# Expert layers in tiles of 256 or 128 slots, sorted by group, with a float32 down projection; half of the attention sums on VectorE

## The chip, the cores and the metric

The kernel runs on one core of a Trainium2 chip. The metric is the device time of one execution in microseconds (us); lower is better. Engines are named as in the profile: PE (TensorE), DVE (VectorE), ACT (ScalarE), POOL (GpSimd) and SP (SyncE, which only issues DMAs here).

## The reference

`x` is 32 sequences of 256 tokens of 128 features, 8192 tokens. One block is a half-weighted mixture of experts, then windowed attention, then the same mixture of experts again:

```
x = x + 0.5 * ffn(layernorm(x))
x = x + attn(layernorm(x))
x = x + 0.5 * ffn(layernorm(x))

ffn:   scores = softmax(x @ Wg + bg)              # 8 experts
       the 2 best experts of each token
       h  = gelu(x @ W1[e] + b1[e])               # 128 -> 512, exact gelu
       eo = h @ W2[e] + b2[e]                     # 512 -> 128
       out = sum of the 2 results, each times its probability
attn:  16 heads of 8 features; token s looks at tokens s-8 .. s
       softmax(q . k / 0.56) over these 9, times v, then @ Wo
```

## The kernel before

The 8192 tokens are four **groups** of 2048 (128 partitions x 16 tokens). There are two **passes** over the experts, f = 0 ahead of the attention and f = 1 behind it.

**Expert pass.** Each token of a group is normalised, its gates and its two experts are found (`route`, on PE, DVE and ACT), and two copies of its row are scattered to a DRAM buffer sorted by expert (`scatter_rows`: 32 indirect DMAs of POOL for a group, 128 rows each). Groups are collected in **parts**, `PARTS = ((0, 1), (2, 3))`; a part has its own sorted buffer, `x_sorted0` or `x_sorted1`. When all rows of a part have landed, `plan` has told on DVE which expert and which rows each **tile** of `SLOT_TILE` = 256 slots has. A part of two groups has 39 tiles, 156 in both passes. For each tile, SP issues a transposing load of 256 rows (`load_x`: value load, DMA_TRANSPOSE, then a small load of the rows' ids); four loads may be ahead. PE makes the up projection (`up`: 12 float16 products of 256 columns, three for each quarter of the hidden units, since `x` and `W1` are each a high and a low float16 part). ACT applies gelu into `h_f` in float32 and casts a high part; DVE subtracts it for the low part (`split_h`, two for a tile, L1347). PE makes the down projection (`down`: 24 float16 products of 128 columns, and one for the bias). DVE multiplies by the gate (`take_y`, L1355), and POOL scatters the result to `y_pairs` in token order (`scatter_y`, L572: two indirect DMAs for a tile, 312 in all). A ring of four `y_sb` buffers lies between the last two.

**Behind a part.** `load_y` waits until every result of the part that holds group g is scattered; `combine` adds the two results to `x` in SBUF.

**Attention**, group after group: `prepare` and `make_qkv`, then eight chunks of two tokens per partition. `multiply_keys` (DVE), sums over the features (PE for the first four chunks, DVE for the others), softmax, `prob_value(c)` (DVE, product of 2 x 9 x 128 elements into `prod`, L1176), `add_window(c)` (PE: nine float32 products with the identity, 256 columns each, add the nine positions in PSUM, L856), `take_o(c)` (DVE, divided by the sum), `turn_o`, `project` (PE) and `add_attention(c)` (DVE, L1204).

**Order.** Each engine runs five streams (routing r, rows h or s, experts e or y, attention a, preparation p). Their interleaving is written out by hand in strings, one letter per step (`PE_ORDER` and so on); `take_turns` walks them. An engine executes its instructions in this order, so a wait of one stream holds the others behind it. In the second pass, `scatter_rows` waits after each four DMAs (`BURST`) until they have landed.

## Time and profile before

| | |
|---|---|
| median of 3 runs | 1198.52 us (1195.54 to 1204.46) |
| the profiled execution | 1194.16 us, its span 1192.4 us |
| mean granted PE clock | 0.866 of full speed |
| PE busy | 871.4 us (73% of the span) |
| DVE busy | 766.5 us (64%) |
| ACT busy | 666.7 us (56%) |
| POOL busy | 665.9 us (56%) |
| indirect DMAs of POOL | 256 of rows, 312 of results |

Busy time counts the instructions themselves; the space between two of them is idle time, whether the engine waits for another or for its own sequencer. No engine is busy all along, so the totals alone do not bound the kernel: the stages must be read one by one. The execution's own time stands 1.8 us above its span, and 4.4 us under the median of the runs.

### The profile page before, as it was taken

To read this page: it belongs to the slowest core of one execution; us is meant where nothing else is said; L and a number is where in the kernel's file an instruction comes from. 1 tells how busy PE (TensorE), PEld (TensorE's weight loads), DVE (VectorE), ACT (ScalarE), POOL (GpSimd) and SP (SyncE) were. 2 spreads that over 40 slices of the span, in tenths; PEclk is the share of its full clock that TensorE was granted. 3 is DMA by queue.
4 is the path that set the end of the run, shared out by engine and by line. 5 is a ranking of instruction groups with operands and counts; after the bars stand their busy time and mean duration, and the time that the engine had idled before them with its cause. 6 is when DMAs were issued, how large, how long until landed. Compare 5 with 4: busy or idle time off the path is not lost.

```text
span 1192.4 us, 25209 instructions
## 1 busy us (share of the span) xinstructions
PE 871.4 (73%) x7573; PEld 708.8 (59%) x7573; DVE 766.5 (64%) x1366; ACT 666.7 (56%) x1408; POOL 665.9 (56%) x595
## 2 busy tenths in 40 slices
PE   1633086529898989998877978979998783298991
PEld 1523065318676767877766656657786662187781
DVE  4565344216457789579996898679875472056664
ACT  4533186419779666267714621367628673197890
POOL 2386677777775313206665305636675765676672
PEclk9755599759999999999987978989998887598996
DMA  8421143224457110002142002113214341146656
GB/s 267 127 82 48 52 99 75 74 60 89 111 113 155 56 28 23 10 14 53 29 134 72 16 1 67 33 43 72 58 43 71 74 99 54 47 84 163 147 126 213
DMA packets 168050, 94.86 MB, mean 80 GB/s; under 512 B 138893, under 2 KB 151738, under 8 KB 167156
## 3 DMA queue, kind: packets, MB, share of 16 engines
q1 hardware_dynamic: 149748, 57.54, 20.8%
q0 software_dynamic: 18176, 35.72, 10.3%
q8 instruction: 70, 1.15, 0.4%
q14 instruction: 56, 0.46, 0.1%
HBM read 25.78 MB, written 50.59 MB: 64 GB/s over the span
## 4 chain that ended last, share of the span: by engine, by line
PE 25%; DVE 16%; issue 8%; POOL 8%; DMA 8%; SPq 4%; ACT 3%; POOLq 0%; ACTq 0%; DVEq 0%
POOL x_sorted L555 7%; PE bank L948 6%; PE bank L927 6%; DMA x_sorted<-hl,slots_all 5%; PE bank L856 5%; PE bank L843 4%; DVE prod L1132 3%; DVE h_hl L1347 2%; DVE prod L1143 2%; SPq L440 2%; PE bank L829 2%; DMA y_in<-y_pairs 2%; DVE prod L1176 2%; ACT h_f L738 1%; POOL y_pairs L572 1%
## 5 line engine op out<-in xcount | busy, mean ns | idle before, releaser
L572 POOL DMA_INDIRECT y_pairs<-y_sb,tile_ids x312 | 363.2, 1164 | 281.8 <-issue 242.8
L555 POOL DMA_INDIRECT x_sorted<-hl,slots_all x256 | 294.6, 1151 | 223.1 <-DVE hl L1027 92.4
L738 ACT ACTIVATE h_f<-bank,b_cols 128x256 f32<-128x256 f32 x624 | 261.2, 469 | 142.4 <-PE bank L927 125.9
L927 PE MATMUL bank<-xsT,w_hl 128*128 128x256 f16 x1872 | 250.8, 285 | 83.5 <-DMA xsT<-x_sorted 70.9
L948 PE MATMUL bank<-w_hl,h_hl 128*128 x3744 | 249.4, 224 | 64.2 <-DVE h_hl L1347 64.1
L1347 DVE TENSOR_TENSOR h_hl<-h_f,h_hl 128x512 f16<-128x512 f32 x312 | 212.2, 687 | 110.1 <-ACT h_hl L744 106.8
L948 PEld LDWEIGHTS bank<-w_hl,h_hl 128*128 128x128 f16 x3744 | 218.5, 100 | 88.0 <-issue 70.3
L927 PEld LDWEIGHTS bank<-xsT,w_hl 128*128 x1872 | 182.2, 102 | 117.1 <-issue 90.3
L744 ACT CAST h_hl<-h_f 128x512 f16<-128x512 f32 x312 | 192.9, 618 | 9.9
L856 PE MATMUL bank<-prod,ident 128*128 128x256 f32 x576 | 143.2, 408 | 16.5 <-DVE prod L1176 15.0
L856 PEld LDWEIGHTS bank<-prod,ident 128*128 128x128 f32 x576 | 116.5, 206 | 37.1 <-DVE prod L1176 18.9
L1355 DVE TENSOR_TENSOR y_sb<-bank,tile_ids 128x256 f32<-128x256 f32 x156 | 65.7, 421 | 80.4 <-issue 45.8
L662 ACT COPY qkv<-bank 128x384 f32<-128x384 f32 (+1 forms) x96 | 41.2, 444 | 77.4 <-PE bank L829 37.0
L1132 DVE TENSOR_TENSOR prod<-qkv 128x2304 f32<-128x2304 f32 x32 | 81.5, 2549 | 0.3
L1176 DVE TENSOR_TENSOR prod<-score,qkv 128x2304 f32<-128x2304 f32 x32 | 81.5, 2548 | 0.1
L843 PE MATMUL bank<-prod,ident 128*128 128x288 f32 x256 | 63.9, 407 | 0.4 <-DVE prod L1132 0.4
L938 PE MATMUL bank<-b_hl,ones_b 64*128 x156 | 44.4, 284 | 20.9 <-DVE y_sb L1355 20.7
L843 PEld LDWEIGHTS bank<-prod,ident 128*128 128x128 f32 x256 | 48.2, 190 | 14.7 <-DVE prod L1132 1.0
L647 ACT CAST hl<-xn_r 128x1024 f16<-128x1024 f32 x20 | 20.8, 1039 | 59.9 <-DMA x_sorted<-hl,slots_all 59.9
L1016 DVE TENSOR_TENSOR hl<-xn_r,hl 128x1024 f16<-128x1024 f32 x20 | 24.4, 1222 | 46.1 <-ACT hl L647 46.1
L938 PEld LDWEIGHTS bank<-b_hl,ones_b 64*128 64x128 f16 x156 | 14.5, 93 | 57.7 <-issue 57.1
L829 PE MATMUL bank<-wqkv,xnT_p 128*128 128x384 f32 x128 | 47.0, 492 | 0.0
(151 smaller groups left out, 825.1 us busy)
## 6 DMA issues: line engine op xcount, KB each, us to landing
y_in<-y_pairs SPq DMA_DIRECT2D x24, 512.0 KB, 4.2
y_pairs<-y_sb,tile_ids POOLq DMA_INDIRECT x312
x_sorted<-no_rows SPq DMA_DIRECT2D x32, 144.0 KB
x_sb<-in_L_attn_x SPq DMA_DIRECT2D x4, 1024.0 KB, 6.3
x_sorted<-hl,slots_all POOLq DMA_INDIRECT x256
qkv<-y_pairs SPq DMA_DIRECT2D x8, 512.0 KB, 6.8
xsT<-x_sorted SPq DMA_TRANSPOSE x156
tile_ids<-x_sorted SPq DMA_DIRECT2D x156, 2.0 KB
```

Of the source, the lines that this page charges most:

```text
L555: pool.indirect_dma_start(out=x_sorted[p], out_offset=bass.IndirectOffsetOnAxis(ap=slots_all[:, at:at + 1], axis=0), in_=hl[:, c % 2, i // ...
L572: pool.indirect_dma_start(out=y_pairs, out_offset=bass.IndirectOffsetOnAxis(ap=tile_ids[:, t.n % IDS, i, 0:1].bitcast(U32), axis=0), in_=y ...
L738: ins = act.activation(h_f[:, u % H_RING, c % 2, :], bank[h_banks.uses[u][0]][:, (c % 2) * 256:(c % 2 + 1) * 256], ACT.Gelu, bias=b1_cols[ ...
L744: act.copy(h_hl[:, t.par, 0, 2 * b:2 * b + 2, :], h_f[:, u % H_RING]).then_inc(h_hi, 1)
L829: pe.matmul(prep_bank[k % PREPS][:, 0:3 * D], xnT_p[:, k - RADIUS, 1:1 + P], wqkv[:], start=True, stop=True).then_inc(qkv_done, 1)
L843: ins = pe.matmul(score_bank[c % 2][:, 0:JH * W * HEADS].rearrange("p (n h) -> p n h", h=HEADS), ident[:], products[:, :, d, :], start=(d ...
L856: ins = pe.matmul(score_bank[c % 2][:, 0:JH * D].rearrange("p (j d) -> p j d", d=D), ident[:], prod[:, c % 2, :, w, :], start=(w == 0), st ...
L927: ins = pe.matmul(dst, w_flat[:, bass.ds((e * HC + c) * (2 * P) + ws * P, P)], xsT[:, t.ring, s], start=(n == 0), stop=(n == 2))
L948: ins = pe.matmul(into[:, half, :], h_hl[:, t.par, hs, c, mine], w_flat[:, bass.ds(at + ws * D, D)], start=False, stop=(c == HC - 1 and ws ...
L1132: ins = dve.tensor_tensor(prod[:, prod_of[c]], q_ap.to_broadcast([P, JH, W, D]), windows(lo, D), ALU.mult)
L1176: dve.tensor_tensor(prod[:, c % 2].rearrange("p j w (h d) -> p j w h d", d=DK), score[:, lo:lo + JH].rearrange("p j w (h o) -> p j w h o", ...
L1347: dve.tensor_tensor(h_hl[:, t.par, 1, 2 * b:2 * b + 2, :], h_f[:, u % H_RING], h_hl[:, t.par, 0, 2 * b:2 * b + 2, :], ALU.subtract).then_i ...
```

## The change

- **Parts.** The first pass has one part for each group; the second has (0, 1), (2) and (3). Seven parts, each with its own buffer, its own `plan` and its own eight tails to clear (of 128 rows, where it was 256).
- **Tiles.** An expert's rows are cut into units of 128. Tiles are wide (two units, 256 slots) or half (one unit). A part of one group has 15 wide and 9 half tiles, the part of two groups has 31 and 9: 184 tiles, 121 wide and 63 half, 305 units in all. `plan` has 34 steps for it, where it had 16.
- **Down projection.** `W2` stays in float32, and so does `h_f`, now a ring of six. The cast on ACT and `split_h` on DVE go; `down` has 8 float32 products of 128 columns for a wide tile and 4 for a half one, in place of 24 in float16.
- **Attention.** For the odd chunks (1, 3, 5, 7) of each group the nine positions are added on DVE by halving (4 + 4, 2 + 2, 1 + 1, and the ninth), four instructions of 1024, 512, 256 and 256 elements behind `prob_value(c)`. `add_window` goes for them on PE.
- **Buffers and orders.** The normalised rows of group 3 lie in `xn_r`, not in `y_in`. All five order strings are new.

```diff
-SPARE = 8
-TAIL = SLOT_TILE
+SPARE = 10
+TAIL = P
-PARTS = ((0, 1), (2, 3))
+H_RING = 6
+SPLITS = (((0,), (1,), (2,), (3,)), ((0, 1), (2,), (3,)))
+SUMMED_BY_DVE = (1, 3, 5, 7)
 POOL_ORDER = (
-    "sssssssssyysyyyyyysyysyysssyyyyyyyyyyyyyyyyyyysyyyyyyyyyyyyyyyyyyyyyyyyyyyyyyyyyyyyyyyyyyyyyyssssssssssssssss"
+    "ssssssyyyyyyysyyyyyyyysyyyyyyyysyyyyyyyyyyysyyyyyyyyysysyyyyyyyyyyyyyyyssyyyssyyyyyyyyyyyyyssssyssssyyyyyyyyy"
...
-    HT = [(2 * GROUP * len(gs) - E) // SLOT_TILE + E for gs in PARTS]
+    UNITS = [(2 * GROUP * len(gs) - E) // P + E for gs in PARTS]
+    WIDE = [(n - E) // 2 for n in UNITS]
+    HT = [n - w for n, w in zip(UNITS, WIDE)]
...
 def experts():            # ACT
-                    for b in range(2):
-                        u = 2 * t.n + b
+                    for b in range(t.halves):
+                        u = t.u + b
                         act.wait_ge(h_done, u + 1)
                         if u >= H_RING:
-                            act.wait_ge(h_split, u - (H_RING - 1))
...
+                            act.wait_ge(y_done, tile_of_unit[u - H_RING] + 1)
...
-                        act.copy(h_hl[:, t.par, 0, 2 * b:2 * b + 2, :],
-                                 h_f[:, u % H_RING]).then_inc(h_hi, 1)
...
 def down(t, e):           # PE
                     for c in range(HC):
-                        if c % 2 == 0:
-                            pe.wait_ge(h_split, 2 * t.n + (c // 2 + 1))
-                        at = (e * HC + (c + E * HC)) * (2 * D)
-                        for ws in range(2):
-                            for half in range(2):
-                                mine = slice(half * P, (half + 1) * P)
-                                for hs in range(2 - ws):
-                                    ins = pe.matmul(into[:, half, :], h_hl[:, t.par, hs, c, mine],
-                                                    w_flat[:, bass.ds(at + ws * D, D)], start=False,
-                                                    stop=(c == HC - 1 and ws == half == 1))
+                        if c % t.per == 0:
+                            pe.wait_ge(h_gelu, t.u + (c // t.per + 1))
+                        for half in range(t.halves):
+                            ins = pe.matmul(into[:, half, :], h_part(t, c // t.per)[:, c % t.per, half * P:(half + 1) * P],
+                                            w2_flat[:, bass.ds((e * HC + c) * D, D)], start=False,
+                                            stop=(c == HC - 1 and half == t.halves - 1))
...
 def prob_value(c):        # DVE
+                    if c in SUMMED_BY_DVE:
+                        parts = prod[:, c % 2]
+                        dve.wait_ge(pv_ready, g * CH + (c + 1))
+                        for n in (4, 2):
+                            at.did(dve.tensor_tensor(parts[:, :, 0:n], parts[:, :, 0:n], parts[:, :, n:2 * n], ALU.add))
+                            at.settle()
+                        at.did(dve.tensor_tensor(parts[:, :, 0], parts[:, :, 0], parts[:, :, 1], ALU.add))
+                        at.settle()
+                        at.did(dve.tensor_tensor(parts[:, :, 0], parts[:, :, 0], parts[:, :, W - 1], ALU.add))
+                        yield
...
 def attention(g):         # PE
-                    yield from add_window(c)
-                    yield from add_window(c + 1)
+                    for k in (c, c + 1):
+                        if k not in SUMMED_BY_DVE:
+                            yield from add_window(k)
...
 def experts():            # DVE
-                def split_h(t, b):
-                    u = 2 * t.n + b
-                    dve.wait_ge(h_hi, u + 1)
-                    dve.tensor_tensor(h_hl[:, t.par, 1, 2 * b:2 * b + 2, :], h_f[:, u % H_RING],
-                                      h_hl[:, t.par, 0, 2 * b:2 * b + 2, :], ALU.subtract).then_inc(h_split, 1)
```

**Where the orders differ.** First place: POOL's queue from its first scatter. A row says which DMAs follow one another and how many; `y_pairs` are results, `x_sortedN` the rows of part N. Before:

```order
L555 DMA x_sorted0<-hl,slots_all 36864x144 x64
L555 DMA x_sorted1<-hl,slots_all 36864x144 x8
L572 DMA y_pairs<-y_sb,tile_ids 16384x128 x4
L555 DMA x_sorted1<-hl,slots_all 36864x144 x8
L572 DMA y_pairs<-y_sb,tile_ids 16384x128 x12
```

The same place in the changed kernel:

```order
L579 DMA x_sorted0<-hl,slots_all 18688x144 x32
L579 DMA x_sorted1<-hl,slots_all 18688x144 x16
L596 DMA y_pairs<-y_sb,tile_ids 16384x128 x16
L579 DMA x_sorted1<-hl,slots_all 18688x144 x8
L596 DMA y_pairs<-y_sb,tile_ids 16384x128 x15
L579 DMA x_sorted1<-hl,slots_all 18688x144 x8
L596 DMA y_pairs<-y_sb,tile_ids 16384x128 x8
```

The 39 results of part 0 are now complete with the 103rd DMA; before, part 0 (78 results, of groups 0 and 1) was complete with the 206th.

Second place: the end of POOL's queue, from the last group's rows in the second pass on. Before, then changed:

```order
L555 DMA x_sorted1<-hl,slots_all 36864x144 x4
L572 DMA y_pairs<-y_sb,tile_ids 16384x128 x2
L555 DMA x_sorted1<-hl,slots_all 36864x144 x28
L572 DMA y_pairs<-y_sb,tile_ids 16384x128 x88
```

```order
L579 DMA x_sorted6<-hl,slots_all 18688x144 x8
L596 DMA y_pairs<-y_sb,tile_ids 16384x128 x21
L579 DMA x_sorted6<-hl,slots_all 18688x144 x8
L596 DMA y_pairs<-y_sb,tile_ids 16384x128 x16
L579 DMA x_sorted6<-hl,slots_all 18688x144 x4
L596 DMA y_pairs<-y_sb,tile_ids 16384x128 x17
L579 DMA x_sorted6<-hl,slots_all 18688x144 x12
L596 DMA y_pairs<-y_sb,tile_ids 16384x128 x45
```

The last 32 rows' DMAs now have 54 results among them and 45 behind them, where 2 lay among them and 88 behind them. Ahead of the first of these rows stand 430 DMAs in the changed queue.

Third place: DVE between the chunks of an attention. Before, in group 0:

```order
L1204 TENSOR_TENSOR x_sb<-bank7,x_sb 128x256
L1176 TENSOR_TENSOR prod<-score,qkv 128x2304
L1185 TENSOR_REDUCE ssum<-score 128x128
L1188 RECIPROCAL sinv<-ssum 128x128
L1347 TENSOR_TENSOR h_hl<-h_f,h_hl 128x512
L1355 TENSOR_TENSOR y_sb<-bank3,tile_ids 128x256
L1347 TENSOR_TENSOR h_hl<-h_f,h_hl 128x512 x2
L1195 TENSOR_TENSOR o_sb<-bank6,sinv 128x256
```

and changed:

```order
L1240 TENSOR_TENSOR x_sb<-bank7,x_sb 128x256
L1194 TENSOR_TENSOR prod<-score,qkv 128x2304
L1203 TENSOR_TENSOR prod<-prod 128x2x512
L1203 TENSOR_TENSOR prod<-prod 128x2x256
L1205 TENSOR_TENSOR prod<-prod 128x2x128
L1207 TENSOR_TENSOR prod<-prod 128x2x128
L1213 TENSOR_REDUCE ssum<-score 128x128
L1216 RECIPROCAL sinv<-ssum 128x128
L1396 TENSOR_TENSOR y_sb<-bank3,tile_ids 128x256
L1231 TENSOR_TENSOR o_sb<-bank6,sinv 128x256
```

The three `h_hl` are gone, and four additions stand behind the product. Between the first product with the keys and the last `add_attention`, DVE has 68 `y_sb` (47 wide, 21 half) where it had 38, 16 `hl` where it had 12, 48 BN_STATS where it had 40, 24 additions of results to `x_sb` where it had 16, and two plans where it had one.

## Rows read from the trace of the kernel before

**Rows 1.** The page, busy time and 40 equal slices (tenths of busy time).
```profile
PE 871.4 (73%) x7573; PEld 708.8 (59%) x7573; DVE 766.5 (64%) x1366; ACT 666.7 (56%) x1408; POOL 665.9 (56%) x595
PE   1633086529898989998877978979998783298991
...
POOL 2386677777775313206665305636675765676672
```

**Rows 2.** Busy time by stretch: from:to, length, busy us (instructions) of five engines, clock, DMA.
```profile
160.00:360.00 200.00, 140.39 (x1616) 115.52 (x1615) 87.33 (x154) 129.09 (x270) 154.68 (x144) 0.85 0.40 89
402.00:892.00 490.00, 430.07 (x2837) 343.09 (x2836) 412.25 (x583) 245.08 (x528) 217.13 (x158) 0.94 0.16 43
520.00:600.00 80.00, 70.42 (x675) 58.72 (x673) 75.35 (x107) 56.56 (x114) 41.85 (x30) 0.99 0.16 36
```

**Rows 3.** Timeline of POOL: start us, us, instruction, idle time before it.
```profile
46.81 1.15 POOL L555 DMA_INDIRECT x_sorted<-hl,slots_all  x1 [37.94 <-DVE hl L1027]
...
142.22 0.96 POOL L555 DMA_INDIRECT x_sorted<-hl,slots_all  x1 [0.30 <-issue]
...
199.82 0.95 POOL L555 DMA_INDIRECT x_sorted<-hl,slots_all  x1 [0.30 <-issue]
...
342.12 0.98 POOL L572 DMA_INDIRECT y_pairs<-y_sb,tile_ids  x1 [0.30 <-issue]
...
595.95 2.48 POOL L572 DMA_INDIRECT y_pairs<-y_sb,tile_ids  x1 [1.40 <-issue]
...
974.80 0.96 POOL L555 DMA_INDIRECT x_sorted<-hl,slots_all  x1 [0.30 <-issue]
...
1030.88 0.96 POOL L555 DMA_INDIRECT x_sorted<-hl,slots_all  x1 [0.30 <-issue]
...
1170.50 0.98 POOL L572 DMA_INDIRECT y_pairs<-y_sb,tile_ids  x1 [0.30 <-issue]
```

**Rows 4.** Timeline of DVE.
```profile
352.64 0.69 DVE L1107 TENSOR_TENSOR x_sb<-y_in,x_sb 128x512 f32<-128x512 f32 x1 [0.69 <-DMA y_in<-y_pairs]
...
402.17 2.56 DVE L1132 TENSOR_TENSOR prod<-qkv 128x2304 f32<-128x2304 f32 x1
...
595.03 2.55 DVE L1176 TENSOR_TENSOR prod<-score,qkv 128x2304 f32<-128x2304 f32 x1
...
891.56 0.88 DVE L1204 TENSOR_TENSOR x_sb<-bank,x_sb 128x256 f32<-128x256 f32 x2
```

**Rows 5.** Timeline of SP's queue; these are the moments of issue.
```profile
148.40 1.26 SPq L440 DMA_TRANSPOSE xsT<-x_sorted  x1
...
151.02 1.24 SPq L440 DMA_TRANSPOSE xsT<-x_sorted  x1
...
1033.92 1.23 SPq L440 DMA_TRANSPOSE xsT<-x_sorted  x1
```

**Rows 6.** The chain of waits: start us, us, what.
```profile
1124.10 1.45 PE bank L948 x24
1125.55 1.31 PE bank L927 x12
...
1127.07 1.45 PE bank L948 x24
```

**Rows 7.** Timeline of PE.
```profile
483.72 1.11 PE L873 MATMUL bank<-wo_sb,oT 128*128 128x128 f32 x8
```

**Rows 8.** Groups of instructions: xcount | busy us, mean ns | idle before.
```profile
L948 PE MATMUL bank<-w_hl,h_hl 128*128 x3744 | 249.4, 224 | 64.2 <-DVE h_hl L1347 64.1
L1347 DVE TENSOR_TENSOR h_hl<-h_f,h_hl 128x512 f16<-128x512 f32 x312 | 212.2, 687 | 110.1 <-ACT h_hl L744 106.8
L873 PEld LDWEIGHTS bank<-wo_sb,oT 128*128 128x128 f32 x128 | 18.3, 209 | 2.8 <-ACT oT L674 1.7
L856 PE MATMUL bank<-prod,ident 128*128 128x256 f32 x576 | 143.2, 408 | 16.5 <-DVE prod L1176 15.0
L1016 DVE TENSOR_TENSOR hl<-xn_r,hl 128x1024 f16<-128x1024 f32 x20 | 24.4, 1222 | 46.1 <-ACT hl L647 46.1
```

More of the change, by code:

```diff
@@ L369, in macaron, with sums_before @@
         SCATTERS = J * DMA
+        def sums_before(g, c):
+            return g * (CH - len(SUMMED_BY_DVE)) + sum(k not in SUMMED_BY_DVE for k in range(c))
         def xt(t, n=1):
@@ L714, in routes @@
                     if q == PARTS[0][-1]:
-                        for part in range(2):
-                            round_weights(part)
-                            yield
+                        round_weights()
+                        yield
             def prepares():
@@ new lines, in plan @@
+                did(dve.tensor_tensor(units[:, 0, :], counts[:], units[:, 1, :], ALU.subtract))
+                for k in range(2):
+                    did(dve.tensor_tensor(m.sums[:, k], earlier[0:1, :].rearrange("o (e f) -> o e f", f=E),
+                                          units[:, k, :].rearrange("o (e f) -> o e f", e=1).to_broadcast([1, e1, E]), ALU.mult))
+                did(dve.tensor_reduce(starts[:].rearrange("o k e -> o (k e)"),
+                                      m.sums.rearrange("o k e f -> o (k e) f"), X, ALU.add))
@@ new lines, in plan @@
+                did(dve.tensor_scalar(counts[:, 0:1], starts[:, 0, E:e1], float(2 * WIDE[p]), None, ALU.max))
+                did(dve.tensor_scalar(starts[:, 1, :], starts[:, 1, :], counts[:, 0:1], None, ALU.add))
+                offs = row_off[:, 1:].rearrange("o (k e) -> o k e", k=2)
+                did(dve.memset(row_off[:, 0:1], 0.0))
+                for k in range(2):
+                    did(dve.scalar_tensor_tensor(out=offs[:, k], in0=starts[:, k], scalar=-float(P), in1=start,
+                                                 op0=ALU.mult, op1=ALU.add))
@@ L1294, in plan @@
+                did(dve.tensor_tensor(m.row, m.row, m.row2, ALU.add))
+                did(dve.scalar_tensor_tensor(out=tile_row[:, cols], in0=m.unit, scalar=float(P),
+                                             in1=m.row, op0=ALU.mult, op1=ALU.add))
+                dve.tensor_tensor(tile_expert[:, cols], m.expert, m.expert2, ALU.add).then_inc(plan_ready, 1)
                 yield
```

373 lines of the change are left out of this document (189 added, 184 removed).

## The prediction

> **What bounds the kernel now.** I read the busy shares first [rows 1]: no engine is above 73%, so the whole is not one engine's work but a row of stages, and the slices show them. For the first two slices no experts run. From then to about 360 us POOL's slices read 7 and 6 while PE's fall to 3 in places: POOL is the pace. The stretch from 160 to 360 us gives the price: 144 indirect DMAs in 200 us, 1.39 us each, with 0.30 us between one and the next even when its data are ready [rows 2, 3]. From 402 to 892 us attention runs; there DVE is busy 412 of 490 us (84%) and PE 430 (88%) [rows 2, 4], both in one chain, so neither can be full. The last stage is experts alone: tile after tile, 1.45 us of down products, 1.31 us of up products and 0.21 us of bias, 2.97 us a tile [rows 6].
>
> Three waits join the stages. Attention can't start until part 0 (groups 0 and 1) is complete: POOL's 206th DMA at 342 us, the first result added at 352.6, the first product of attention at 402 [rows 3, 4]. From the last `add_attention` at 892 to the first rows of group 3 it takes 83 us, mostly because the routing steps stand between expert steps; the 32 rows take 56 us, four at a time [rows 3]. And then 39 tiles have to go through before the end: SP's first load of the last part is at 1033.9, 158 us ahead of it [rows 5].
>
> **The change, part by part.**
>
> The start: `plan` now stands ahead of the gates' copy that releases POOL, and has 34 small instructions, so I add 7 us to the first scatter at 46.8 (34 at 0.2 us, an estimate: 256 elements take 0.44, and these have 1 to 216). Part 0 is complete with the 103rd DMA, not the 206th. The 103rd stood at 199.8 in the run before [rows 3]; with 7 us more, 207. From there to the first addition it took 10.5 us (342.1 to 352.6), to the first product another 49.5 [rows 3, 4]; with ACT and PE less full I take 48. Attention starts at 265 us instead of 402. Nothing else in this change is worth as much, 137 us.
>
> Attention itself, on DVE. Its 412 us lose `split_h`: 38 tiles lay in the stretch, two at 0.687 us each, 52 us [rows 8]. They gain the halving: 1024, 512, 256 and 256 elements. A two-input instruction of 1024 elements took 1.22 us [rows 8], of 512 0.69 and of 256 0.44 [rows 4], so 2.8 us a chunk and 45 us for sixteen. 47 wide and 21 half `take_y` at 0.44 and at most that, less the 38 there now, give 10; four more `hl` 5; one more set of statistics 5; eight more additions of results 6; the other plan 7. That makes 412 - 52 + 45 + 33 = 438 us. On PE it loses 16 chunks of nine products, half of 143 us, 72 us [rows 8]. A tile on PE costs 1.31 + 0.95 + 0.21 = 2.5 us when wide and half of it when half: eight float32 products of 128 columns ran in 1.11 us from first start to last end, the last alone being 0.28 of it, so 0.12 us each [rows 7], where 24 in float16 take 1.45. The 30 tiles more cost PE what the cheaper ones save (68 at 2.1 us, 143, against 38 at 3.4, 129), so 430 - 72 + 14 = 372 us. PE stops being a rival to DVE. Its slack and the missing round trip over PE for half of the chunks should cut DVE's idle time of 78 us in this stretch to some 50: the four attentions take 488 us and end at 753. This idle time is the term I know least; at 84% busy as now it would be 521 us, at 95% 461.
>
> POOL beside it. From 265 us, with 145 DMAs done (42 more at 1.39), 285 must go before group 3's last rows, in the new order. At 1.39 us that is 396, and 24 bursts of the second pass wait 2 us each (56 us for 32 rows and two results, 34 at 1.27 being 43), 48: 709 us. But beside attention POOL is slower: between 520 and 600 us 30 DMAs were busy 41.85 us, 1.40, with the 0.30 1.70 us each [rows 2]; one that met a product of 2.55 us on DVE took 2.48 instead of 0.98 [rows 3, 4]. At 1.70 it is 798 us. The halving adds to such instructions, 45 us, the going of `split_h` takes away 52. So POOL comes to that place between 709 and 798, and attention (below) at 793: near a tie, and attention is at the late end, so I let attention decide and keep the other as a rival.
>
> The Trainium skill (SBUF — State Buffer, "Who interferes with whom") says that a DVE instruction with two SBUF inputs contends with GpSimd's reads, and that whichever issues first keeps the other out; this is a rule against the halving. The row of 2.48 us beside the product agrees with it. By the rule the change would be neutral here, as 52 us of such instructions go and 45 come.
>
> The end. From the last `add_attention` to the first rows: 83 us now; in the new order some nine PE steps of experts stand ahead of the routing, and then one or two between its steps, so I take 40 (statistics, 16 normalisations, routing: about 30 us of dependent steps; the bound above is 83). First rows at 793. The 32 rows take 56 us as now; 54 results lie among them at 1.28 us, 69: 918 us. Loads begin 3 us behind (1030.9 to 1033.9) [rows 3, 5]. The last part has 24 tiles, not 39. PE needs 2.5 us for a wide one, POOL 2.6; SP's own queue issued a tile each 2.62 us (148.40 to 151.02) [rows 5] and does so for a half one too, unless the transposing load of 128 rows is issued faster. So 23 x 2.6 = 60 us to the last load, 981; some 6 us for that tile's way over four engines (estimate: 3 to land, and one product stage, gelu, product, gate of under 1 us each). From the last scatter to the end it was 21.9 us [rows 3]; four chunks of two additions at 0.69 go, 5.5 [rows 4], 16.4. Sum 1003.7 us of span, 1005.5 with the 1.8 outside. Against the run of before that is -189: 137 by the earlier start, 2 by attention, 43 by the routing and 76 by the smaller last part, less 69 for the results that now lie among the last rows. I forecast 1005 us; the profiled run lies 4 us under the median, well inside the range.
>
> What costs nothing: ACT loses its casts, and is the bound nowhere (56% busy [rows 1]); if it had been full, they would count. The 56 tails instead of 32, each of half the size, stand in SP's queue ahead of a part's first load, in time that waits for the rows; at the borders in the second pass they may cost up to 10 us each when the rows are already there.
>
> **Rivals.**
> - *Attention runs fuller.* DVE at 95%, the routing in 30 us and 15 us less from first results to first product: 250 + 461 + 30 = 741 us, 52 less, 954 us. For it: PE has slack. Against: 84% is what this chain reached, and POOL must be at its quick end (709).
> - *POOL is the bound beside attention.* `take_y` may not overtake the scatter by more than four tiles, so DVE, which runs attention in the same queue, is held behind POOL. At 1.70 us it comes to group 3's rows at 798, and the 86 DMAs there cost 86 x 1.70 + 16 = 162, not 125: 1005 + 5 + 37 = 1047 us. For it: 285 DMAs at 1.7 fill the time. Against: 1.39 where DVE was not full.
> - *The early start does not come.* SP has the loads of group 0's results behind 30 tile loads, six of them of part 1, whose tails and rows it must wait for. If the queue holds them until 402 us as now, only the end is cheaper: 1194 - 43 - 76 = 1075 us, the results being out of the way by then.
> - *The float32 rule.* Rows show twice the time of float16 for a column: 576 products of 256 columns were busy 143.2 us, 0.25 each [rows 8], 12 in float16 took 1.31, 0.11 each [rows 6]. With four times, a product of 128 columns takes 0.21 us and a wide tile 3.2 on PE: PE is as full as now beside attention (68 tiles at 0.7 more, 420 of 488), DVE back at 84%, +33, and the last part's wide tiles +9: 1047 us. The Trainium skill (FP8 and Floating Point Precision, "TensorE Precision Notes") has it that true float32 takes four passes through the array; the trace has two times, and its measurement decides.
> - *Slower than before.* The down products could fail to hide their weight loads, since here each has new weights: a load of 0.21 and a product of 0.28 in series, 0.49 us [rows 7, 8]. 1220 of them take 598 us against 249 now [rows 8]; PE: 871 - 249 - 72 + 598 = 1148 us, and at 93% busy 1234 us. It passes the time of before from 0.46 us a product. Against it: `project` has new weights for each product too, and ran at 0.12.
>
> **How the numbers follow.** The forecast has 0.50, its own range 970 to 1040 (the attention between 461 and 521 us, the routing 30 to 60). Fuller attention 0.20, POOL 0.15, no early start 0.07, the float32 rule 0.05, slower 0.03. To leave out no more than 2 in 10 the range has to take in 954 and 1047 with their own spread: 935 to 1075. No change within 1%, which is about what a measurement of this kernel can tell, has no case of its own; I give it 0.01, slower 0.03 and faster 0.96.
>
> **What the new profile would show.** The first product of attention near 265 us; the last `add_attention` near 753; DVE in between 88% to 90% busy; POOL without long idle times from 55 to 790 us; down products of a wide tile in 0.95 us; the last part's loads from about 920 us, 2.6 us apart. Wrong would be: attention starting past 300 us, POOL at 1.7 us throughout, DVE waiting on scattered results, or a float32 product dearer than 0.2 us.

## The result, and the profile after

The changed kernel takes 1103.11 us (median of 4 runs, 1100.78 to 1108.01) against 1197.47 us of the kernel before: ratio 0.921, 95% interval 0.917 to 0.926. The forecast was 1005 us with a range of 935 to 1075. The sign was right; the forecast was 98 us too low, and the time lies above the range. The profiled execution has a span of 1102.5 us, 98.8 more than the 1003.7 of the sum. Ratios, here and below, leave out executions that took over 1.5% longer than the fastest of the same kernel, so a few in the table of experiments aren't the quotients of the medians beside them.

The page after, to be read beside [rows 1]: busy time, 40 slices, and then some of its groups.

```profile
PE 878.7 (80%) x6345; PEld 736.0 (67%) x6345; DVE 642.4 (58%) x1305; ACT 498.3 (45%) x1217; POOL 669.1 (61%) x593
PE   1542996899989888987999679689889577992994
...
POOL 3076777667857787466677256367757664574553
...
L963 PE MATMUL bank<-w_sb,h_f 128*128 x2440 | 337.9, 291 | 0.9 <-ACT h_f L758 0.9
...
L871 PE MATMUL bank<-prod,ident 128*128 128x256 f32 x288 | 73.7, 412 | 5.9 <-DVE prod L1194 3.3
```

PE was expected to have less to do than before and has more, 878.7 us for 871.4. The reason stands in the count of L963. The code makes 1220 float32 products there (305 units, four quarters), and the trace has 2440 records. L871 has 288 records for 144 products. So a float32 product is two PE instructions in the trace. The same was to be seen in the kernel before: 576 records at L856 [rows 8] are 32 chunks of nine products, 288.

The chain of waits in the last part, beside [rows 6]: start us, us, what.

```profile
1057.86 0.21 PE bank L957
1058.07 1.98 PE bank L963 x16
1060.05 1.31 PE bank L946 x12
...
1076.50 1.09 PE bank L963 x8
1077.59 0.67 PE bank L946 x12
1078.26 0.16 PE bank L957
```

A wide tile is 1.98 + 1.31 + 0.21 = 3.50 us of PE, dearer than before's 2.97 and not the 2.5 of the forecast. The 16 records of 1.98 us are eight products, 0.25 us each. A half tile is 1.09 + 0.67 + 0.16 = 1.92 us, where the forecast had half of 2.5.

POOL's timeline at the places of [rows 3]: the first row, the 103rd DMA, the first and the last row of the last group, the last result.

```profile
53.86 4.36 POOL L579 DMA_INDIRECT x_sorted<-hl,slots_all  x1 [44.53 <-DVE hl L1043]
...
201.07 0.98 POOL L596 DMA_INDIRECT y_pairs<-y_sb,tile_ids  x1 [0.30 <-issue]
...
862.89 0.97 POOL L579 DMA_INDIRECT x_sorted<-hl,slots_all  x1 [0.30 <-issue]
...
1006.08 0.96 POOL L579 DMA_INDIRECT x_sorted<-hl,slots_all  x1 [0.30 <-issue]
...
1087.75 0.98 POOL L596 DMA_INDIRECT y_pairs<-y_sb,tile_ids  x1 [0.34 <-issue]
```

DVE's timeline, beside [rows 4]: first result added, first product of attention, last `add_attention`.

```profile
212.66 0.69 DVE L1123 TENSOR_TENSOR x_sb<-y_in,x_sb 128x512 f32<-128x512 f32 x1 [0.49 <-DMA y_in<-y_pairs]
...
276.63 2.55 DVE L1148 TENSOR_TENSOR prod<-qkv 128x2304 f32<-128x2304 f32 x1
...
815.35 0.87 DVE L1240 TENSOR_TENSOR x_sb<-bank,x_sb 128x256 f32<-128x256 f32 x2 [2.41 <-PE bank L890]
```

Busy time by stretch, beside [rows 2]: attention, the way to the last group's rows, those rows, the last part.

```profile
276.00:816.00 540.00, 469.27 (x2984) 380.51 (x2983) 446.12 (x691) 249.21 (x585) 339.57 (x245) 0.93 0.24 61
816.00:863.00 47.00, 38.02 (x315) 32.96 (x314) 20.46 (x78) 27.62 (x65) 31.20 (x32) 0.95 0.29 69
863.00:1006.00 143.00, 107.06 (x925) 92.24 (x925) 31.33 (x74) 50.93 (x146) 85.09 (x85) 0.89 0.44 113
1006.00:1088.00 82.00, 74.20 (x633) 64.41 (x633) 14.95 (x34) 34.08 (x96) 44.66 (x46) 0.92 0.45 100
```

With these views the span can be set out stage by stage, each stage by its two ends:

| stage, us | before | forecast | after |
|---|---|---|---|
| start to the first product of attention | 402.2 | 265 | 276.6 |
| to the last `add_attention` | 490.2 | 488 | 539.6 |
| to the last group's first rows | 82.4 | 40 | 46.7 |
| these 32 rows | 56.1 | 125 | 143.2 |
| to the last result | 139.6 | 69 | 81.7 |
| to the end of the span | 21.9 | 16.4 | 14.8 |

The early start came, 126 of its 137 us. Half of what is missing lies in attention (52 us), where DVE's busy time is near the forecast (446 for 438) and PE's is not (469 for 372).

### The profile page after: what moved, and what is told of

The parts are those of the page before. It is cut to its first block, busy times and chain, and to the rows that moved or that the text cites. A ratio compares the mean times of both kernels' runs of the same rounds, so it can differ in the third digit from the quotient of the medians.

```text
span 1102.5 us, 22490 instructions
## 1 busy us (share of the span) xinstructions
PE 878.7 (80%) x6345; PEld 736.0 (67%) x6345; DVE 642.4 (58%) x1305; ACT 498.3 (45%) x1217; POOL 669.1 (61%) x593
## 3 DMA queue, kind: packets, MB, share of 16 engines
q0 software_dynamic: 17952, 35.71, 10.5%
## 4 chain that ended last, share of the span: by engine, by line
PE 21%; DVE 12%; POOL 10%; DMA 8%; issue 8%; SPq 2%; ACT 0%; POOLq 0%; DVEq 0%; ACTq 0%
PE bank L963 11%; POOL x_sorted L579 8%; PE bank L946 6%; DMA x_sorted<-hl,slots_all 5%; POOL y_pairs L596 2%; DVE prod L1194 2%; DMA y_pairs<-y_sb,tile_ids 1%; DVE prod L1159 1%; PE bank L957 1%; DVE prod L1148 1%; PE bank L871 1%; DVE y_sb L1396 1%; SPq L466 1%; DVE prod L1203 1%; DVE smax L1180 1%
## 5 line engine op out<-in xcount | busy, mean ns | idle before, releaser
L758 ACT ACTIVATE h_f<-bank,b_cols 128x256 f32<-128x256 f32 (+1 forms) x736 | 263.9, 438 | 348.0 <-PE bank L946 337.9
L579 POOL DMA_INDIRECT x_sorted<-hl,slots_all x256 | 308.1, 1204 | 183.2 <-issue 76.1
L963 PE MATMUL bank<-w_sb,h_f 128*128 x2440 | 337.9, 291 | 0.9 <-ACT h_f L758 0.9
L963 PEld LDWEIGHTS bank<-w_sb,h_f 128*128 128x128 f32 x2440 | 300.6, 199 | 20.7 <-issue 1.9
L946 PE MATMUL bank<-xsT,w_hl 128*128 128x256 f16 (+1 forms) x2208 | 246.9, 262 | 18.7 <-DMA xsT<-x_sorted 12.6
L1396 DVE TENSOR_TENSOR y_sb<-bank,tile_ids 128x256 f32<-128x256 f32 (+1 forms) x184 | 68.9, 375 | 293.7 <-PE bank L963 237.0
L946 PEld LDWEIGHTS bank<-xsT,w_hl 128*128 x2208 | 196.2, 101 | 46.9 <-issue 23.5
L957 PE MATMUL bank<-b_hl,ones_b 64*128 x184 | 48.7, 265 | 68.7 <-DVE y_sb L1396 67.3
L957 PEld LDWEIGHTS bank<-b_hl,ones_b 64*128 64x128 f16 x184 | 17.1, 93 | 107.6 <-issue 104.4
L871 PE MATMUL bank<-prod,ident 128*128 128x256 f32 x288 | 73.7, 412 | 5.9 <-DVE prod L1194 3.3
L871 PEld LDWEIGHTS bank<-prod,ident 128*128 128x128 f32 x288 | 58.9, 211 | 15.7 <-DVE prod L1194 3.5
L858 PEld LDWEIGHTS bank<-prod,ident 128*128 128x128 f32 x256 | 48.0, 190 | 14.0 <-DVE prod L1148 0.9
L671 ACT CAST hl<-xn_r 128x1024 f16<-128x1024 f32 x24 | 25.0, 1047 | 62.9 <-DMA x_sorted<-hl,slots_all 62.9
L614 ACT ACTIVATE xn_r<-x_sb,shift_r,rstd_r 128x128 f32<-128x128 f32 x96 | 38.4, 484 | 18.5 <-DVE shift_r L1019 18.5
```

The costliest lines, as they stand in the source:

```text
L579: pool.indirect_dma_start(out=x_sorted[p], out_offset=bass.IndirectOffsetOnAxis(ap=slots_all[:, at:at + 1], axis=0), in_=hl[:, c % 2, i // ...
L758: ins = act.activation(h_part(t, b)[:, k, :], bank[h_banks.uses[u][0]][:, k * t.slots:(k + 1) * t.slots], ACT.Gelu, bias=b1_cols[:, bass.d ...
L858: ins = pe.matmul(score_bank[c % 2][:, 0:JH * W * HEADS].rearrange("p (n h) -> p n h", h=HEADS), ident[:], products[:, :, d, :], start=(d ...
L871: ins = pe.matmul(score_bank[c % 2][:, 0:JH * D].rearrange("p (j d) -> p j d", d=D), ident[:], prod[:, c % 2, :, w, :], start=(w == 0), st ...
L946: ins = pe.matmul(dst, w1_flat[:, bass.ds((e * HC + c) * (2 * P) + ws * P, P)], slots_of(t)[:, s], start=(n == 0), stop=(n == 2))
L957: pe.matmul(into, ones_b2[:], b2_hl[:, bass.ds(e * D, D)].rearrange("k (o d) -> k o d", o=1) .to_broadcast([2 * B2_LO, t.halves, D]), star ...
```

## Experiments

Besides two controls there were 16 runs of nine kernels, in five sessions, each on another chip. In three of these sessions the kernel before took 1338 to 1351 us instead of 1197, and their runs are compared only within such sessions, by their ratio to the kernel before. The control, which is the changed kernel itself, took 1102.75 us in the second session (ratio 0.921) and 1105.76 us in the fourth (0.921):

> The changed kernel itself, as the control of the runs beside it: the four runs so far came in a session in which the kernel before took 1347 us where it had taken 1197, and their profiles show idle times of up to 14 us on several engines at once that the first profiles do not have, so each needs the changed kernel of its own session. If the slower session stretches every kernel alike, the ratio to the kernel before is again 0.92. If it costs something for each wait or instruction fetched, it may lie anywhere between 0.90 and 0.94.

> The changed kernel as control. In a session in which the kernel before takes 1197 us: 1103, ratio 0.921. In one in which it takes some 1350 us (two sessions were so): if such a session stretches every kernel alike, 0.92 too, 1241 us, and then the POOL load costs nothing (0.914 and 0.918), half of the down products save 2 to 3% and float16 products save nothing; if it is kinder to the changed kernel, some 0.90, 1215 us, with the POOL load costing 1.5%.

| session | kernel | us | ratio to before (95%) |
|---|---|---|---|
| 2 (before 1197.6) | float32 down alone | 1199.6 | 1.001 (0.999 to 1.004) |
| 2 | DVE's sums alone | 1210.8 | 1.012 (1.005 to 1.018) |
| 2 | both | 1209.8 | 1.010 (1.007 to 1.013) |
| 4 (before 1197.1) | half of the down products | 1085.7 | 0.907 (0.903 to 0.911) |
| 4 | float16 down, 16 products | 1086.5 | 0.906 (0.902 to 0.910) |
| 4 | load on POOL | 1118.1 | 0.931 (0.926 to 0.936) |
| 1 and 3 (before 1347, 1351) | half of the down products | 1213.8, 1219.4 | 0.891, 0.900 |
| 1 and 3 | float16 down | 1240.0, 1245.0 | 0.919, 0.925 |
| 1 and 3 | load on POOL | 1236.1, 1232.8 | 0.918, 0.914 |
| 1 and 3 | sums back on PE | 1294.5, 1300.5 | 0.962, 0.963 |
| 5 (before 1338) | float16 down, no halving | 1227.9 | 0.918 (0.913 to 0.922) |
| 5 | float16 down, waits after eight rows | 1238.2 | 0.924 (0.920 to 0.928) |

**The two edits alone, on the kernel before.** The float32 down projection alone:

```diff
-                        for ws in range(2):
-                            for half in range(2):
-                                mine = slice(half * P, (half + 1) * P)
-                                for hs in range(2 - ws):
-                                    ins = pe.matmul(into[:, half, :], h_hl[:, t.par, hs, c, mine],
+                        for half in range(2):
+                            ins = pe.matmul(into[:, half, :], h_f[:, (2 * t.n + c // 2) % H_RING, c % 2, half * P:(half + 1) * P],
+                                            w2_flat[:, bass.ds((e * HC + c) * D, D)], start=False,
```

> The kernel before with the float32 down projection alone: W2 and h in float32, a ring of six for h, no cast on ACT and no subtraction on DVE; tiles, parts, sums and orders as before. Theory (a float32 product of 128 columns is two PE instructions and 0.25 us): a tile on PE goes from 2.97 to 3.50 us, 156 tiles or 83 us of PE time more, 212 us of DVE time less. PE was 88% busy beside attention, so the time stays the same or grows: ratio to the kernel before 1.00 to 1.04. As the prediction priced it (0.12 us): a tile 2.5 us, ratio 0.94 to 0.97. If DVE was what held attention, the 52 us that it loses there show in spite of the dearer products: 0.96 to 0.99.

DVE's sums alone (the four halving additions, and `add_window` gone for the odd chunks), and both together:

> The kernel before with the sums of the odd chunks on DVE alone: PE loses 72 us beside attention, DVE gets 45 more (412 to 457 of 490 us). Theory: with the float16 down projection DVE is then the fuller one, 93%, and the time is the same or a little longer: ratio 0.99 to 1.03. Rival (PE and the way over it are the bound of attention): ratio 0.95 to 0.97.

> The kernel before with both, float32 down projection and DVE's sums, so without parts of one group, half tiles and new orders. PE beside attention 430 - 72 + 20 = 378 us, DVE 412 - 52 + 45 = 405: both have room, attention some 20 to 30 us shorter, the last part of 39 tiles 21 us longer. Theory: ratio 0.98 to 1.01, and what is missing to the 0.92 of the changed kernel is the parts' and the orders' share. Rival (float32 and the sums are the gain, the parts little): 0.93 to 0.95.

For the sums on DVE the order strings are those of the kernel before, so DVE's additions and PE's empty steps stand where its old work was laid out.

Attention in these three, from the first product to the last addition, as windows of the float32 kernel, of the one with DVE's sums, and of both:

```profile
402.00:891.00 489.00, 442.20 (x2527) 360.54 (x2525) 369.01 (x506) 198.39 (x449) 211.43 (x157) 0.94 0.16 43
```

```profile
404.00:916.00 512.00, 392.57 (x2549) 303.48 (x2549) 455.68 (x647) 245.21 (x526) 223.64 (x161) 0.86 0.16 42
```

```profile
400.00:900.00 500.00, 400.77 (x2247) 317.59 (x2246) 412.26 (x571) 199.74 (x451) 220.75 (x156) 0.88 0.16 42
```

The float32 down projection takes 43 us from DVE, gives PE 12, and attention has the length it had [rows 2]. DVE's sums take 37 us from PE, give DVE 44, and attention is 22 us longer. With both edits PE has 29 us less to do than before (400.8 for 430.1) and DVE the same (412.3), and attention, expected 20 to 30 us shorter, is 10 us longer. Neither edit is a gain by itself, nor are both, in the orders of the kernel before. The granted clock of the two kernels with DVE's sums is 0.86 and 0.88 in these windows, beside 0.94; its part in the added length was not separated. What is missing to the changed kernel, 1209.8 - 1102.75 = 107 us, is due to the rest of the change taken together: parts of one group, half tiles and the new orders. Their shares weren't tried apart; the new orders are also laid out for the two edits, so what these are worth in them is not in the 1.010.

**Half of the down products.** In the changed kernel; its results lack half of the hidden units:

```diff
-                        for half in range(t.halves):
+                        for half in range(t.halves if c % 2 else 0):
```

> The changed kernel with half of its down projection left out: of the four quarters of the hidden units only the second and fourth are multiplied with W2, so the results lack the other half. 610 float32 products go; nothing is added, and no engine but PE has less to do. Its down stage of a wide tile should then take 1.0 us, which is what the prediction had priced for the whole of it. Theory PE: a float32 product of 128 columns costs 0.25 us and not 0.12, PE is busy 469 of 540 us beside attention and sets the pace there and in the last part. Then attention loses 40 us or more, the end some 35 to 45, and the kernel takes 1005 to 1035 us. Rival POOL: its queue (24 groups of four rows that wait, 1.7 us a DMA beside attention) sets the pace, and the kernel stays at 1080 to 1103 us. Rival DVE: DVE, busy 446 of 540 us, can't be used fuller; the end gains some 35 us and attention nothing, 1065 us.

> The changed kernel with half of its down projection left out (its results lack half of the hidden units). Beside its control: theory PE, the ratio to the control is 0.92 to 0.95; rival POOL or DVE, above 0.965.

In the fourth session it saved 20.0 us (1105.76 to 1085.74), 1.8%, a fourth to a third of what the PE theory gave; the ratio to the control, 0.982, lies where the rivals had it. This kernel has the number of down products halved, about what the prediction had priced for them (1.09 us for a wide tile in its chain), so its profile shows much of what the rest of the prediction missed. Windows of the control, and of the kernel with half of the products:

```profile
276.00:821.00 545.00, 470.68 (x2977) 380.12 (x2977) 446.10 (x690) 249.23 (x585) 339.00 (x244) 0.92 0.24 60
821.00:870.00 49.00, 36.90 (x320) 32.08 (x318) 20.68 (x77) 27.50 (x65) 31.26 (x32) 0.92 0.28 67
870.00:1011.00 141.00, 106.92 (x925) 92.19 (x925) 31.49 (x76) 50.93 (x146) 84.75 (x85) 0.90 0.44 115
1011.00:1093.00 82.00, 73.69 (x633) 64.16 (x633) 14.83 (x34) 33.98 (x96) 45.29 (x46) 0.93 0.44 100
```

```profile
271.00:803.00 532.00, 431.64 (x2511) 332.87 (x2510) 444.20 (x689) 249.55 (x586) 338.42 (x244) 0.90 0.24 61
803.00:853.00 50.00, 40.56 (x255) 32.94 (x253) 20.69 (x74) 28.17 (x65) 31.70 (x32) 0.76 0.28 69
853.00:987.00 134.00, 89.31 (x697) 70.93 (x697) 31.98 (x78) 51.15 (x146) 84.81 (x86) 0.82 0.47 120
987.00:1064.00 77.00, 60.86 (x473) 48.51 (x473) 14.56 (x34) 34.17 (x96) 45.07 (x47) 0.88 0.47 107
```

Attention gives up 39 us of PE's work and 13 us of time. Its down products alone are 52 us less busy there (78.7 for 130.5), and other groups of PE got dearer. The granted clock is lower than the control's in every stretch (0.90, 0.76, 0.82, 0.88 for 0.92, 0.92, 0.90, 0.93), so the saving is that of fewer products at a lower clock. With PE at 81% and DVE at 83% neither is full, and the stage is still 44 us longer than the forecast's 488. The chain of waits of this kernel in the middle of attention shows one place where it is held:

```profile
681.03 0.95 POOL x_sorted L579
681.98 0.31 issue
682.29 1.07 POOL x_sorted L579
683.36 0.30 issue
683.66 0.95 POOL x_sorted L579
684.61 0.30 issue
684.92 2.30 DMA x_sorted<-hl,slots_all
687.26 0.76 issue
...
692.86 2.28 DMA x_sorted<-hl,slots_all
695.22 1.05 ACT hl L671
696.36 1.08 issue
697.44 0.17 DVE hl L1036
697.61 2.46 DVE prod L1148
```

POOL scatters four rows, waits 2.3 us until they have landed and 0.76 us more, and scatters the next four. When the buffer of `hl` is free, ACT fills it, DVE subtracts, and the product of attention behind it in DVE's queue starts. So here the rows of the next pass hold DVE, and with it attention. Whether fewer such waits make attention shorter is asked by the last run below. The waits of DVE in the stretch (us in total, times, the longest) have it first:

```profile
DVE hl L1032 <- ACT hl L671: 30.4, 7, 8.4
DVE score L1169 <- PE bank L858: 14.3, 7, 4.7
```

**The same down stage in float16.** h is rounded to float16 by gelu itself, W2 has a high and a low part; 16 products of 128 columns for a wide tile:

```diff
-        h_f = sb("h_f", [P, H_RING, 2 * SLOT_TILE], F32)
+        h_f = sb("h_f", [P, H_RING, 2 * SLOT_TILE], F16)
...
-                        for half in range(t.halves):
-                            ins = pe.matmul(into[:, half, :], h_part(t, c // t.per)[:, c % t.per, half * P:(half + 1) * P],
-                                            w2_flat[:, bass.ds((e * HC + c) * D, D)], start=False,
-                                            stop=(c == HC - 1 and half == t.halves - 1))
+                        for ws in range(2):
+                            for half in range(t.halves):
+                                ins = pe.matmul(into[:, half, :], h_part(t, c // t.per)[:, c % t.per, half * P:(half + 1) * P],
+                                                w2_flat[:, bass.ds((e * HC + c) * (2 * D) + ws * D, D)], start=False,
+                                                stop=(c == HC - 1 and ws == 1 and half == t.halves - 1))
```

> The changed kernel with the down projection in float16 in another form than before's: gelu writes its result in float16 (no low part, no subtraction on DVE, no cast on ACT), W2 is split once into a high and a low float16 part, so a wide tile has 16 float16 products of 128 columns. Before's 24 took 1.45 us; 16 should take 0.97 us, as half of the float32 products do. It computes h with the rounding of float16, else everything. Theory PE: as the run with half of the down projection, 1005 to 1035 us. Rival (it is not PE's time, but something else of the changed kernel): 1080 us or more. If this one is slow and the run with half of the products fast, the number of PE instructions counts and not their time.

> The changed kernel with 16 float16 products of 128 columns a wide tile, at 0.97 us in place of 1.98. In two sessions it was 2.5 to 2.8% of the kernel before slower than the run with half of the float32 products, though its down stage takes the same time. If PE's time in the down stage decides: the same as half_down_3 within 1%, ratio to the control 0.92 to 0.95. If the number of instructions decides: between 0.97 and 1.01 of the control.

1086.5 us, the same as with half of the float32 products (ratios 0.906 and 0.907), with twice the records there and the same busy time of PE in all (795.5 and 794.2 us). So in the fourth session PE's time counts, and not the number of its instructions, although the size, 0.983 of the control, is much smaller than the 0.92 to 0.95 that this theory gave. Its group in the page:

```profile
L967 PE MATMUL bank<-w_hl,h_f 128*128 x2440 | 199.3, 230 | 1.3 <-ACT h_f L761 1.0
```

As many records as in the changed kernel, and 138.6 us less busy (337.9 there). It is the fastest kernel of the study that computes every term, 1.7% below its control (1086.54 to 1105.76), at the price of an h of less precision. In sessions 1 and 3 it was behind the other by 2.5 to 2.8% of the kernel before by the ratios, by 1.9% by the medians of all executions; why the two differ there is open.

**Load on POOL.**

```diff
+                        if spares[0]:
+                            pool.wait_ge(spare_step, spares[0])
+                        pool.iota(spare_p[:], [[1, P]], base=0, channel_multiplier=1).then_inc(spare_step, 1)
+                        spares[0] += 1
                         pool.indirect_dma_start(
```

> The changed kernel with one more instruction on POOL ahead of each scattered result: 305 times an iota of 128x128 into a buffer that nobody reads. One of this size took 0.36 us in the changed kernel's trace, so POOL gets some 110 us of work and perhaps 0.1 us more of queue for each. Rival POOL (its queue beside attention is the pace): most of it is paid, 1180 us or more. Theory PE: POOL has slack (busy 340 of 540 us beside attention, its idle time there mostly waits for results); only the start up to the first part's completion pays, 39 results at 0.4 us or 16 us, and the tail little: 1105 to 1130 us.

> The changed kernel with an iota of 128x128 on POOL ahead of each of the 305 scattered results, 0.45 us of queue each, some 137 us in all. Theory PE: ratio to the control 1.00 to 1.025, the start later by 39 times 0.45 or 15 us at most. Rival POOL: 1.05 or more.

12.4 us more than its control (1118.14 to 1105.76), 1.1%, for this group:

```profile
L601 POOL IOTA spare_p<- 128x128 int32 x305 | 80.2, 263 | 96.3 <-issue 45.4 <-DMA x_sorted<-hl,slots_all 26.8 <-DVE y_sb L1403 23.1
```

80 us of work, with 45 us of idle time ahead of it that is put down to its queue, cost 12. Between the two profiles, attention differs by 2 us (276.5 to 823 us, control 276.5 to 821), the last group's rows by 8 (874.4 to 1023.0 us, control 870.2 to 1011.2), the way to them by 2. POOL's scattering of results is no bound beside attention; its bursts of rows, a wait in itself, are another matter and weren't touched by this.

**The sums of the odd chunks back on PE.** `SUMMED_BY_DVE = ()`, with the steps of the orders kept.

> The changed kernel, but PE adds the nine positions of the odd chunks too, as before, and DVE's halving (four instructions, 2.8 us a chunk) goes; the steps of all orders stay where they are. PE gets 144 float32 products more, 72 us; DVE has 45 us less. Theory PE (PE is the fuller engine beside attention, 469 of 540 us): attention grows by 50 to 80 us, 1155 to 1185 us. Rival DVE (the products with two inputs and DVE's queue set the pace): 1060 to 1100 us. If both are in one chain and neither is full, 1103 to 1130 us.

> The changed kernel with the odd chunks' sums back on PE (72 us of PE more, 45 us of DVE less), once more in a usual session; in the slow one its ratio to the kernel before was 0.962. PE is the fuller engine beside attention: attention 40 to 70 us longer, 1145 to 1175 us. If DVE or the way through both engines is the bound: 1090 to 1120 us.

There is no control in sessions 1 and 3, but the kernel with the load on POOL is the control with more to do: against it the sums on PE cost 4.8% and 5.3% (0.9618 to 0.9177, 0.9627 to 0.9139), 58 and 68 us there. Attention of the load's kernel, then of this one, in the third session:

```profile
353.00:916.00 563.00, 465.76 (x2975) 374.78 (x2974) 444.86 (x690) 248.96 (x585) 366.24 (x360) 0.92 0.23 58
```

```profile
358.04:994.00 635.96, 542.94 (x3284) 437.74 (x3282) 403.80 (x627) 250.63 (x586) 319.95 (x251) 0.92 0.21 52
```

77 us more of PE's work are 73 us more of time, although DVE has 41 less. What was added to PE is paid nearly whole; of what was taken away in the fourth session (39 us) a third came back. PE wasn't full, though: it was busy 83% of the stretch without this work and 85% with it. What came back is the way over PE: DVE's waits for these sums ahead of `o_sb` (L1234) took 61.2 us in 14 places here, and the kernel with the load shows none of them among its nine largest. The halving on DVE, no gain in the kernel before with its orders, is one here.

**No halving.** The kernel with the float16 down stage, without the four additions:

> The kernel with 16 float16 products a wide tile (1086.5 us), and the four halving additions of the odd chunks left out: these chunks' results lack eight of the nine positions. DVE has 45 us less beside attention (444 to 399), PE and POOL the same (PE some 432 of 532 us). Theory DVE: attention is DVE's work at 83 to 84% busy, whatever else changes, 399/0.835 = 478 us, 54 less: 1030 to 1045 us. Rival (the steps between the engines, or PE, set its length, and DVE's share falls): 1065 to 1087 us.

The ratio is 0.918 where the same kernel with the halving had 0.919 and 0.925 in sessions 1 and 3. Attention took 560 us (350.7 to 911) with DVE busy 403, and 556 us in session 3 with DVE busy 446. The kernel of the next run, which has the halving, took 1238.2 us in the same session, 10 more than this one's 1227.9. The DVE theory, which gave 54 us, falls: of 43 us less of DVE's work some 10 were given back, if the next run's own edit changed nothing. This is from sessions in which attention takes some 25 us longer than in the others; that it would be so in those too was not tried.

**Waits after eight rows.** The same kernel, in the second pass POOL waits after eight DMAs instead of four:

```diff
-                        if f and (i + 1) % BURST == 0:
+                        if f and (i + 1) % (2 * BURST) == 0:
...
```

> The kernel with 16 float16 products a wide tile (1086.5 us), and in the second pass POOL waits for the landing of the rows after eight DMAs, no longer after four; the order is the same. A wait takes some 2.3 to 3 us; 16 of 32 go, four of them among the last group's rows. Theory: the last rows come 10 us earlier and the time falls by as much, 1072 to 1080 us; beside attention nothing changes. Rival (POOL waits for results of DVE there, the wait is only taken over): 1083 to 1088 us.

0.924, between the 0.919 and 0.925 of the kernel that waits after four: no gain that can be told. The last group's rows took 154.0 us (986.35 to 1140.37) where they took 159.3 in session 3, so half of the expected 10 us may be there, but not in the time; this profile is of the kernel's slowest execution (1247.63 us), which makes the comparison weak. In attention POOL's waits for landed rows fell from 26.3 us (12 of them, session 3) to 9.0 (4), and attention took 562 us (352.1 to 914.1) where it took 556 in session 3 and 558 in session 1. So the place shown above, where a burst of rows holds DVE, is not what sets attention's length in these sessions. DVE waited for `hl` less there too, 8.2 us in session 3 against 27.3 for the same kernel in session 4, so for the usual sessions this is not settled.

## Why the prediction was wrong

The steps whose size failed are these, the largest first.

**"Its slack and the missing round trip over PE for half of the chunks should cut DVE's idle time of 78 us in this stretch to some 50."** This step failed. DVE was idle 540 - 446 = 94 us. It is not only a consequence of the dearer product: with half of the down products gone, PE was idle for 100 us, and DVE's idle time was still 88; with both edits in the kernel before it was 88 too, beside 99 us of idle PE. DVE's waits in attention, before and after, show what became of the missing round trip:

```profile
DVE o_sb L1195 <- PE bank L856: 21.8, 10, 3.5
DVE hl L1016 <- ACT hl L647: 12.5, 4, 5.8
DVE y_sb L1355 <- PE bank L948: 2.0, 3, 1.0
```

```profile
DVE hl L1032 <- ACT hl L671: 24.2, 6, 5.8
DVE y_sb L1396 <- PE bank L963: 19.3, 16, 3.3
DVE o_sb L1231 <- PE bank L871: 4.8, 3, 4.0
```

The wait for the sums on PE fell by 17 us, as the prediction said. But waits for down products ahead of `y_sb` (17 us more) took their place, and those for `hl` grew by 12. With both edits in the kernel before it was the same: 1.1 us for the sums, 30.8 for the down products. The prediction took DVE as the engine that attention is made of, and its idle time as something that another engine's slack would fill. The runs show neither: DVE with 43 us less (float32 alone, and 12 more for PE) left attention as long, and without the halving it was as long too (sessions 5 and 3). PE with 77 us more made it 73 longer. The two engines wait for each other, for ACT and for the rows, in a written-out order. Of the 88 us with half of the products, the wait for `hl` (30.4 us) is the largest one seen; that these waits are a matter of the order is argued, since no other order was tried. The prediction gave a bound for this term, 521 us at 84%, and 84% was what the trace of before had. That end was the nearer one; DVE was busy 83% of 540 us.

**"Eight float32 products of 128 columns ran in 1.11 us ..., so 0.12 us each."** The eight rows of [rows 7] are four products: `project` makes two for each chunk, 64 in all, and the group counts 128 records. A product takes 0.25 us, and a wide tile's down stage 1.98 us, not 0.95. [rows 8]'s "576 products of 256 columns" are 288, 0.51 us each by the chain of the half kernel (18 records, 4.57 us). So a column in float32 costs 0.25/0.055 = 4.5 times one in float16 (12 products of 256 columns in 1.31 us, 0.055 for 128 columns). The rival "the float32 rule" had it, with a chance of 0.05: the two times that the prediction set against it were a miscount. The Trainium skill (FP8 and Floating Point Precision, "TensorE Precision Notes") says that true float32 takes four passes through the array, and the trace agrees with 4.5. Worth of this term: 20.0 us of the 98, measured by the half kernel. The rival's 42 us were too much for it: it charged attention 33 us, and 13 came.

The 372 us of PE had a second fault. They put the old tile at its recorded busy time in the stretch (3.4 us) and the new one at the time of back-to-back products in a chain (2.5), where [rows 6] has 2.97 for the old. In the half kernel the groups of the expert tiles (L946, L963, L957) were busy 198 us in attention, not 143, and PE in all 432.

**The sum by the kernel with half of the products.** Its span is 1078.3 us, 74.6 above the forecast: attention 532 for 488 (+44), the first product at 271.5 for 265 (+6.5), 50 us to the last group's rows for 40 (+10), the rows 134 for 125 (+9), to the last result 76 for 69 (+7), and the tail 14.9 for 16.4 (-1.5). That is 75. The other 24.2 lie between this profile and the 1102.5 of the first one, taken in another session; for the products the medians of one session give 20.0.

**The start** was right in size. Part 0 was complete at 201 (forecast 207), since POOL's first 103 DMAs were closer together; the first addition came at 212.7 (217); but from there to attention it took 64 us and not 48. "With ACT and PE less full" holds for ACT (38.6 of 64 us from 212 to 276, before 44.8 of 50 from 352 to 402) and not for PE (61.0 of 64, before 44.4 of 50).

**POOL.** The 285 DMAs before group 3's last rows were to be done between 709 and 798 us. In attention they were busy 339.57/245 = 1.39 us each, so the prediction's 1.40 was right; but POOL was idle 200 of 540 us there, and more work for it left attention as long, so it was not the bound, and the rival with its 1047 us did not come as priced. The last group's rows took 143 us and not 125. There POOL waited 16.8 us in five places for rows to land (before: 15.8 in seven), and 10.5 us in seven for results of DVE, which the forecast had at nothing.

**The last part.** The transposing load was issued in 1.2 us for a half tile too, and in the last part PE set the pace, and not SP: 3.50 and 1.92 us a tile, 74.2 of 82 us busy.

**The early start, the routing and the sign** came as forecast: 126 of 137 us, 36 of 43, and no slower case.

## What to carry to other kernels

Before a price is taken from a merged row of PE, count the products in the code and divide the row by that number, not by its count of records. Don't price a new tile in one measure (back-to-back products of a chain) against an old one in another (busy time in a stretch). Don't take an engine's idle time away because another engine gets slack: name the wait that goes, and ask which wait comes in its place; here 17 us went and 29 came. The busy share that the stage had before (84%) was nearer than any better one. Splitting the work into smaller parts, so that the next stage starts when the first part is complete, was worth 107 us with half tiles and new orders, while the two edits that moved work between engines cost 1% without it.

## What the runs showed of the hardware

In these profiles a float32 product of 128 by 128 by 128 shows as two records and takes 0.25 us of PE (16 records in 1.98 us); each record of its weight load has 199 ns in the mean (L963), where a float16 one has 101 (L946). A DMA_TRANSPOSE of 128 rows took SP as long to issue as one of 256, 1.2 us. With less for PE to do, its granted clock was lower: 0.82 for 0.90 in the last group's rows with half of the down products, 0.88 for 0.94 in attention with both edits in the kernel before. In the sessions in which the kernel before took 1338 to 1351 us, the profiles have idle times that the other sessions don't have: with the float16 kernel, POOL's 20.8 us ahead of 123.6 and 12.2 ahead of 155.6 (session 3) are its longest between 60 and 360 us. Its first product of attention came at 352 us, and at 273 in session 4, while attention itself took 556 us for 531. Sessions and chips changed together, and the cause was not looked for.
